# Grouped attention in a four-layer kernel: GpSimd's low-half subtractions cut into pieces of 512 columns

## The reference

```python
q = (hidden_states @ q_proj_w.T)            # 32 heads of 128, 512 -> 4096
k = (cross_attention_states @ k_proj_w.T)   # 8 key/value heads of 128
v = (cross_attention_states @ v_proj_w.T)
q = rmsnorm(q, q_norm_w); k = rmsnorm(repeat(k, 4), k_norm_w)
scores = einsum('bhqd,bhkd->bhqk', q, k) * scale + attention_mask
attn = softmax(scores)
out = einsum('bhqk,bhkd->bhqd', attn, repeat(v, 4))
x = x + out @ o_proj_w.T
```

## Time and profile before

| What | Value |
|---|---|
| time, median of 3 runs | 872.14 us (871.28 to 873.34) |
| span of the profiled execution | 875.2 us |
| PE busy | 783.4 us (90%) |
| DVE busy | 719.1 us (82%) |
| ACT busy | 519.3 us (59%) |
| POOL busy | 428.5 us (49%) |

### The profile page before, as it was taken

How to read it: one execution, slowest core, us unless ns; L and a number is a source line. 1 busy time by engine, 2 the same in 40 slices (tenths; PEclk the granted TensorE clock), 3 DMA queues, 4 the chain that set the end, 5 groups by cost and what they waited for, 6 DMA issues and landing times. The chain is left out here.

```text
span 875.2 us, 16429 instructions
## 1 busy us (share of the span) xinstructions
PE 783.4 (90%) x5146; PEld 634.7 (73%) x5146; DVE 719.1 (82%) x1732; ACT 519.3 (59%) x1408; POOL 428.5 (49%) x380
## 2 busy tenths in 40 slices
PE   1976899858987999999999999999999999578878
PEld 0474676534776898898898897898898898465446
DVE  7878998968788888888888888887887887955974
ACT  6864898747466756756656756756656656321421
POOL 3237087805226647646646746646646746531110
PEclk9999999979999999999999999999999999789899
DMA  8253246562203102102102202201200300103001
GB/s 304 93 193 121 75 150 207 163 187 80 96 2 97 50 26 95 50 24 96 48 24 80 64 24 74 70 24 52 92 24 28 116 24 25 48 25 117 1 0 49
DMA packets 39114, 68.23 MB, mean 78 GB/s; under 512 B 5729, under 2 KB 18593, under 8 KB 38946
## 3 DMA queue, kind: packets, MB, share of 16 engines
q1 hardware_dynamic: 39074, 67.73, 23.5%
HBM read 62.38 MB, written 5.34 MB: 77 GB/s over the span
## 5 line engine op out<-in xcount | busy, mean ns | idle before, releaser
L1966 ACT ACTIVATE layer_attention_probs<-xnT,stats 128x512 f32<-128x512 f32 x128 | 93.9, 734 | 137.8 <-DVE stats L2075 137.8
L2244 DVE TENSOR_SCALAR_CACHE_REDUCE xn<-ctxT,candidate 128x512 bf16<-128x512 f32 x240 | 168.8, 741 | 0.0
L1750 PE MATMUL bank<-layer_attention_keysT,layer_attention_queriesT 128*128 128x512 f32 x384 | 122.6, 428 | 5.0 <-DVE layer_attention_queriesT L2068 5.0
L2087 DVE TENSOR_TENSOR layer_attention_probsT<-bank,layer_attention_probsT 128x512 fp32r<-128x512 f32 x128 | 88.0, 688 | 39.8 <-ACT layer_attention_probsT L1974 38.3
L1750 PEld LDWEIGHTS bank<-layer_attention_probsT,layer_attention_values 128*128 128x128 f32 x768 | 99.7, 191 | 23.0 <-DVE layer_attention_probsT L2087 9.3
L1750 PE MATMUL bank<-layer_attention_probsT,layer_attention_values 128*128 128x256 f32 x768 | 103.4, 284 | 14.0 <-DVE layer_attention_probsT L2087 13.9
L1750 PE MATMUL bank<-layer_attention_wo,layer_attention_headsT 128*128 128x512 f32 x384 | 104.5, 417 | 3.0 <-issue 3.0
L1974 ACT CAST layer_attention_probsT<-bank 128x512 fp32r<-128x512 f32 x128 | 74.7, 584 | 50.4 <-PE bank L1826 50.1
L1696 POOL TENSOR_TENSOR layer_attention_mixed<-layer_attention_mixed,xnT 128x512 f32<-128x512 f32 x32 | 52.1, 1627 | 86.3 <-DMA xnT<-inverse_sums 82.8
L1750 PE MATMUL bank<-layer_attention_l_wq,layer_attention_xnT 128*128 128x512 f32 x384 | 93.5, 392 | 0.0
L1750 PE MATMUL bank<-layer_attention_l_wkv,layer_context_parts 128*128 128x256 f32 x720 | 90.5, 278 | 0.0
(11 more groups left out here) (322 smaller groups left out, 1673.0 us busy)
## 6 DMA issues: line engine op xcount, KB each, us to landing
layer_attention_l_raw_qo<-in_wqT SPq DMA_DIRECT2D x9, 1024.0 KB, 5.1
xnT<-inverse_sums SPq DMA_DIRECT2D x16, 512.0 KB, 3.7
layer_attention_l_raw_qo<-in_woT SPq DMA_DIRECT2D x8, 1024.0 KB, 7.1
tw_raw<-in_w_gateT SPq DMA_DIRECT2D x8, 688.0 KB, 5.2
tw_raw<-in_w_upT SPq DMA_DIRECT2D x8, 688.0 KB, 4.2
tw_raw<-in_w_downT SPq DMA_DIRECT2D x6, 768.0 KB, 4.7
layer_attention_l_raw_kv<-in_wkvT SPq DMA_DIRECT2D x9, 512.0 KB, 4.8
ternary<-tw_rounded SPq DMA_DIRECT2D x8, 344.0 KB, 2.6
```

The lines of the kernel that those rows point to most:

```text
L1750: last = pe.matmul(out, stationary[f][a], moving[f][b], start=f == 0 and x == 0, stop=f == count - 1 and x == 2)
L1966: a.activation(probs[:, u % 3, :], masked[:, u % 2, :], ACT.Exp, bias=negmax[:, u:u + 1], scale=-1.0, accum_out=sums[:, u:u + 1]).then_inc ...
L2087: v.tensor_tensor(probsT[:, 1, p % 2, :, columns], T[u % 2][:, :].rearrange("p (c q) -> p c q", c=CPB), probsT[:, 0, p % 2, :, columns], A ...
L2244: own(k.nc.vector.tensor_scalar((k.flags if flags is None else flags)[:, r % 2], row_tile(k.ctxT, r), k.candidate[:, r:r + 1].bitcast(F32) ...
```

## The change

Each subtraction of a low half on GpSimd is issued as two to four instructions of 128x512 in place of one of 128x1024 or 128x2048. The data, the order on GpSimd, the waits and the semaphore counts stay; the increment is now on the last piece. (The first group's weights are prepared earlier by `first_group_split`, L1527 for the queries, which was in pieces already.)

```diff
                 def kv_weights_low(step):
                     g.wait_ge(gw.kv_high, group(step) + 2)
-                    g.tensor_tensor(wkv[:, 1], gw.raw_kv[:, :, :], wkv[:, 0], ALU.subtract).then_inc(gw.kv_low, 1)
+                    for f in range(0, KT, 2):
+                        last = g.tensor_tensor(wkv[:, 1, f:f + 2], gw.raw_kv[:, f:f + 2, :], wkv[:, 0, f:f + 2], ALU.subtract)
+                    last.then_inc(gw.kv_low, 1)
 
                 def q_weights_low(step):
                     g.wait_ge(gw.q_high, group(step) + 2)
-                    g.tensor_tensor(wq[:, 1], gw.raw_q[:, :, :], wq[:, 0], ALU.subtract).then_inc(gw.q_low, 1)
+                    for f in range(KT):
+                        last = g.tensor_tensor(wq[:, 1, f], gw.raw_q[:, f, :], wq[:, 0, f], ALU.subtract)
+                    last.then_inc(gw.q_low, 1)
 
                 def o_weights_low(step, half):
                     heads = slice(half * REP // 2, (half + 1) * REP // 2)
                     if half == 0:
                         g.wait_ge(S_["o_high"], group(step) + 1)
-                    g.tensor_tensor(wo[:, 1, heads], raw_o[:, heads], wo[:, 0, heads], ALU.subtract)\
-                     .then_inc(S_["o_low"], 1)
+                    for h in range(REP)[heads]:
+                        last = g.tensor_tensor(wo[:, 1, h], raw_o[:, h], wo[:, 0, h], ALU.subtract)
+                    last.then_inc(S_["o_low"], 1)
```

## The result

The changed kernel takes 878.77 us (median of 22 runs, 874.14 to 883.29), the kernel before 872.61 us (22 runs, 867.41 to 879.48) beside it. The ratio is 1.0066, with a 95% interval of 1.005 to 1.0083: slower by 0.66%, about 5.8 us by the ratio and 6.2 by the medians.

What follows compares the result with a forecast made beforehand. The prediction took PE to bound the loop and DVE the last step. Its terms 3.1 + 2.6 + 0.2 + 0.2 = 6.1 us, added to the kernel's time, gave 878 us, with 80 in 100 on 873 to 882.

Steps and rivals of the forecast that it cites:

- Length on POOL: Query-weight subtraction on GpSimd: 1.30 us a piece, four take 5.06 us, 0.44 us more than one instruction.
- Who gets in between: At a boundary between two GpSimd pieces one DVE instruction passes, then POOL takes the shared port pair back at once.
- The step that named these four: DVE's bisection update: its four small instructions with two SBUF inputs are the ones POOL can hold up.
- Query weights, 7 x 0.44 = 3.1 us: Seven loop groups with an update: it ends 0.44 us later in each, delaying DVE and PE, 3.1 us in all.
- The hits, 2.6 us and 0.2: Update meeting the multiplication of the heads (L1696): two more groups cost 2.6 us, three already hit 0.2 us.
- Output and key/value weights, 0: Updates during output weights end within 0.1 us of before; key/value weights meet no update; counted as 0.
- Last step, 0.2 us: DVE's choice in the last step: one instruction passes per piece, so nearly the same end; 0.2 us together.
- A: Rival: the update slips through at one boundary, faster, 868.6 to 871 us or about 860; 8 in 100.
- B: Rival: no change, two collisions fewer by a different draw hide 2.6 to 2.8 us, 872 to 874; 12 in 100.
- C: Rival: each small instruction meets one hold more, 1.5 to 2 us in each of seven groups, 882 to 885; 15 in 100.

Runs made afterwards that it cites:

- q_only: Kernel before with only the query weights' subtraction cut into four pieces; 878.2 us, ratio 1.0071 to the kernel before.
- q_eight: Kernel before with the query weights' subtraction cut into eight instructions of 128x256; 885.76 us, ratio 1.0136 to the kernel before.
- gated kernels: Kernel before and changed kernel, each with GpSimd's wait for `add_out` put ahead of the multiplication of the heads (the gate); means 870.67 and 873.63 us.
- after_skip: Changed kernel without the last pair's unread key/value and query low-half subtractions; 877.34 us, ratio 1.006 to the kernel before.
- kv_o_only: Kernel before with only the key/value and output weights' subtractions cut; 871.53 us, ratio 0.9983 to the kernel before.

## Why the prediction was right

The forecast was 878 us, 6.1 us more than before; measured were 878.77 and 5.8 to 6.2 more.

*Length on POOL.* Right: 1.30 us a piece, 5.03 to 5.05 us for four in groups 2 to 7 against a forecast of 5.06 (5.22 in the last step, where DVE's instructions of 256 columns run between the pieces). Eight of 256 took 5.61 against 5.8 by the line.

*Who gets in between.* Right for the four instructions with two SBUF inputs: one per boundary, also when they are small (q_only's first group, q_eight). The step that named these four as the only ones that POOL can hold up was too narrow: `bits`, with one SBUF input, was held 1.63 us in q_eight, and L2279 was held as well. It made no difference to the sum: in the trace of before all 31 `bits` took their bare 0.17 us.

*Query weights, 7 x 0.44 = 3.1 us.* Right: 0.43 us a group by the distances, 2.96 us by the times of the gated kernels.

*The hits, 2.6 us and 0.2.* Near in sum, 3.0 us (2.2 by the ratios), but not in the way that was worked out, so that the total of 6.1 us came out this close is in part luck. The forecast left the inverse sums' arrival where it was and let the window grow over it, which gave five or six hits of seven and 11 to 12 us of waits. The trace had one hit and 5.3 us. In groups 2 to 7 of the kernels with the query weights cut and no gate (the changed kernel, q_only, after_skip) 6 of 18 groups were hit; in those with the query weights whole (before, kv_o_only), 5 of 12. So the traces do not show hits more frequent; they show them dearer. A hit lengthens the distance to the next group by 1.35 to 1.41 us in the five cases before, and by 1.30 to 1.40 in three of the six after. In the other three (481.45 in the changed kernel, one in q_only, one in after_skip) PE's clock fell behind the wait, and the distance grew by 2.9 to 3.1 us (below). No step of the prediction had this. With these shares and prices hits would cost 4.0 us before and 5.0 after in seven groups, 1.0 of the 3.0 us; the traces are too few to place the rest.

*Output and key/value weights, 0.* Right within the noise: 0.9983, and no wait of PE at the updates during the output weights.

*Last step, 0.2 us.* Its first wait was 3.80 us against 3.55, but the second was shorter: PE's second product with the values starts 16.82 us after the last query-weight work in the one trace and 16.83 in the other. So no cost is seen there; the timed runs can't resolve such a sum.

*The rivals.* A fell by the time of the changed kernel and by q_eight. B's lucky draw (fewer hits) did happen to the one profiled execution, whose 876.36 us is still not "no change". C, a hit in every group, did not come about. (The prediction gives the forecast's own range once as 874 to 882 and once as 874 to 881; the measured time lies in both.)

The fastest kernels are those of before with the gate: 870.67 us as the mean of 24 runs with it alone, 2.2 us under the kernel before; 870.53 with the update moved as well (12 runs) and 870.19 with the last step's unread work left out (12 runs) are not told apart from it.

## What to carry to other kernels

Where an engine holds another up by whole instructions, look at what waits: one instruction alone is let go sooner by shorter pieces (`enough` during the output weights took 1.18 us in place of 2.28, though no run was faster by it), a chain of small dependent ones does not, since one of them passes per boundary and each piece adds its fixed cost (here about 0.15 us) before the last of the chain is let go. Order, not size, was the remedy that worked here: a wait that keeps the other engine's next instruction off the chain cost nothing that the traces show (65.84 us between groups with the gate, as without it and without a hit). And with waits that come and go from run to run, compare the distances of equal steps and the gated kernels, not the spans of two traces.

## What the runs showed of the hardware beyond that

*A wait of PE of about 2 us can cost more than itself.* Busy times by stretch (columns as in the earlier trace rows) of the changed kernel around the hit and around a group without one, then of q_only behind its first hit:

```profile
479.40:481.40 2.00, 0.02 (x1) 0.00 (x0) 2.00 (x4) 0.00 (x0) 1.13 (x2) 1.00 0.91 268
481.40:484.40 3.00, 2.95 (x14) 2.95 (x15) 2.90 (x8) 1.29 (x3) 1.54 (x2) 0.50 0.42 165
...
549.20:552.20 3.00, 2.98 (x25) 2.98 (x26) 2.90 (x8) 1.56 (x4) 2.75 (x4) 1.00 0.83 287
```

```profile
348.00:351.00 3.00, 3.00 (x16) 3.00 (x17) 2.90 (x8) 1.66 (x4) 1.49 (x2) 0.59 0.52 197
...
417.20:420.20 3.00, 2.97 (x25) 2.97 (x26) 2.90 (x8) 1.56 (x4) 2.21 (x3) 1.00 0.49 191
```

After 2.03 us of idleness the granted clock was 0.50, that is 1.2 and not 2.4 GHz, in the 3 us that follow, and PE made 14 products where it makes 25. The distance to the next group was 69.21 us instead of 66.27, of which the longer wait explains 1.45 and the clock the other 1.5. In q_only a wait of 1.86 us was followed by 0.59, and one of 1.92 us by 1.00: which of them loses the clock is not settled by their length. Behind the waits of 0.6 us, and behind the five hits of before and kv_o_only with 1.49 to 1.55 us, it was not seen. So in these traces the clock was lost only behind hits of kernels with the cut.

*Not every GpSimd instruction with two inputs holds DVE.* Timelines of POOL and DVE in the kernel before:

```profile
562.18 1.01 POOL L1683 TENSOR_TENSOR layer_attention_ssq<-layer_attention_ssq,minus_half 128x4 f32<-128x4 f32 x1
...
562.51 0.17 DVE L2301 TENSOR_TENSOR candidate<-found,bits 128x8 int32<-128x8 int32 x1
```

`candidate` runs at its bare 0.17 us inside L1683, which raises four columns to the power of minus one half and takes 1.01 us. The same holds in all seven groups of this trace, and in the seven of the changed kernel, where `candidate` is issued 0.10 us into that instruction. So not every GpSimd instruction holds DVE up for its whole length. Here the measurement differs from the rule quoted under q_eight, and the measurement decides. That such an instruction reads its few columns early and computes for the rest of its time is a guess from this, not tried.
